# Input products of four recurrence steps at a time, accumulated in the steps' own PSUM bank and opened by a bias product

## What is computed

```python
x1 = x + (softmax(mask(q @ k.T / sqrt(32))) @ v) @ w_proj + b_proj      # q, k, v = x @ w_qkv + b_qkv, per head
for t in range(512):                                                    # all 8 sequences at once
    h = tanh(h @ Wh + x1[:, t] @ Wx + b)                                # h starts as the image row
    y[:, t] = h
out = x1 + y
```

## Time and profile before

| | us |
|---|---|
| median of 3 runs (1750.9 to 1755.51) | 1754.62 |
| the profiled execution | 1745.16 |
| its span in the trace | 1743.3 |
| TensorE busy | 1610.0 (92%) |
| VectorE busy | 884.2 (51%) |
| ScalarE busy | 707.1 (41%) |
| GpSimd busy | 151.5 (9%) |

### The profile page before, as it was taken

One profiled execution on the slowest core, in us unless ns is written; L12 is line 12 of the kernel. 1 busy time (PEld: TensorE's weight loads), 2 busy tenths in 40 slices (PEclk: granted clock), 3 DMA queues, 4 the chain that ended last, 5 costly groups with the idle time before them and its releaser, 6 DMA issues.

```text
span 1743.3 us, 67044 instructions
## 1 busy us (share of the span) xinstructions
PE 1610.0 (92%) x28908; PEld 1341.3 (77%) x28908; DVE 884.2 (51%) x2954; ACT 707.1 (41%) x2205; POOL 151.5 (9%) x248
## 2 busy tenths in 40 slices
PE   5799999989999999989999999999999998999997
PEld 4678887778787778878877787777777787888886
DVE  4345455555555555555655565556566573222222
ACT  2355555344343445444444444445445452111111
POOL 0110111010100110010101101011010100000000
PEclk8889999999999999999999999999999999999999
DMA  7656566434444465545546466556656560000000
GB/s 247 178 154 177 171 177 178 125 114 132 128 110 124 120 166 135 152 124 150 139 127 161 120 165 160 143 152 163 160 136 163 152 142 24 18 16 22 22 16 22
DMA packets 228438, 221.61 MB, mean 127 GB/s; under 512 B 22952, under 2 KB 187048, under 8 KB 227632
## 3 DMA queue, kind: packets, MB, share of 16 engines
q1 hardware_dynamic: 211568, 175.86, 37.9%
q0 software_dynamic: 16576, 41.46, 8.4%
HBM read 141.45 MB, written 75.76 MB: 125 GB/s over the span
## 4 chain that ended last, share of the span: by engine, by line
PE 76%; DVE 8%; DMA 4%; issue 4%; ACT 4%; SPq 2%; POOL 0%; DVEq 0%; POOLq 0%; ACTq 0%
PE rec L935 25%; PE turned L857 9%; PE dense L392 7%; PE dense L393 6%; PE dense L394 6%; PE scores L849 4%; PE pv L870 4%; PE scores L935 4%; PE dense L905 3%; DVE pre L762 3%; ACT hist L605 3%; PE pv L888 2%; DMA kq<-kq_dram 2%; DMA x_dram<-x1nat 1%; DVE pre L765 1%
## 5 line engine op out<-in xcount | busy, mean ns | idle before, releaser
L935 PE MATMUL rec<-wh,hist 128*8 128x128 f32 x14336 | 481.4, 275 | 63.5 <-ACT hist L605 56.5
L935 PEld LDWEIGHTS rec<-wh,hist 128*8 128x8 f32 x14336 | 353.7, 94 | 151.7 <-ACT hist L605 105.6
L605 ACT ACTIVATE hist<-pre 128x32 f32<-128x32 f32 x512 | 131.7, 257 | 587.7 <-DVE pre L772 352.3
L563 ACT ACTIVATE probs<-probs,nmax 128x128 f32<-128x128 f32 (+3 forms) x512 | 287.7, 562 | 176.0 <-DVE nmax L697 166.9
L697 DVE CUSTOM_DVE_ANT_0 probs<-scores,msk,nimg 128x128 f32<-128x128 f32 (+3 forms) x512 | 275.4, 544 | 52.2 <-PE scores L849 50.2
L762 DVE STREAM_TRANSPOSE pre<-rec 128x128 f32<-128x128 f32 x448 | 141.3, 315 | 316.2 <-PE rec L935 313.4
L857 PE MATMUL turned<-ident,probs 128*128 128x128 f32 x1280 | 241.1, 288 | 2.2 <-DVE probsT L706 1.3
L849 PE MATMUL scores<-kq 96*128 96x128 f32 (+3 forms) x512 | 202.8, 401 | 16.2 <-DMA kq<-kq_dram 15.8
L857 PEld LDWEIGHTS turned<-ident,probs 128*128 128x128 f32 x1280 | 145.2, 141 | 64.8 <-issue 54.4
L570 ACT COPY probsT<-turned 128x128 f32<-128x128 f32 (+3 forms) x256 | 107.6, 420 | 157.5 <-PE turned L857 156.3
L706 DVE COPY probsT<-turned 128x128 f32<-128x128 f32 (+3 forms) x256 | 124.6, 487 | 87.9 <-PE turned L857 87.1
(11 more groups left out here) (160 smaller groups left out, 2224.8 us busy)
## 6 DMA issues: line engine op xcount, KB each, us to landing
kq<-kq_dram SPq DMA_DIRECT2D x96, 320.0 KB, 5.0
kq<-kq_dram SPq DMA_DIRECT2D x96, 256.0 KB, 4.4
...
kq_dram<-qs_hi SPq DMA_DIRECT2D x128, 128.0 KB, 2.0
kq_dram<-ks_hi SPq DMA_DIRECT2D x128, 128.0 KB, 2.7
...
```

What stands on the lines that cost most here:

```text
L563: act.activation(probs[:, g % PROBS, 0:n], probs[:, g % PROBS, 0:n], ACT.Exp, scale=-1.0, bias=nmax[:, e, h:h + 1], accum_out=rowsum[:, e, ...
L605: act.activation(hist[:, g // HALF % 2, :, :, g % HALF], pre[:, :, 0:B], ACT.Tanh).then_inc(h_ready, 1)
L935: last = pe.matmul(d[Q * j:Q * j + B, 0:P], hist[:, before // HALF, f, :, before % HALF], wh[:, f, P * j:P * j + P], start=f == 0 and not ...
```

## The change

The products of x1 with Wx no longer go through VectorE, nor (in blocks 0 to 2) through a `dense` bank and ScalarE. They are accumulated in the bank in which the steps accumulate their state products, for a group of four steps (`GROUP`) at once: row z of each 8 x 4 rows in a column group belongs to step 4k + z. Kind "xsteps" does this for a whole group k in the attention stage, right ahead of the group's first step; "xpart" does a quarter of the next group's after each step of the tail. The bank is opened (start=True) by 4 matmuls of a row of ones (one partition, 32 columns) with the bias row `brow`, then 16 matmuls of `wx` with 32 columns of x1 accumulate. Every step then accumulates 16 matmuls with a stationary tile of 32 columns, of which 24 are zero (`state_tile`), so that it changes its own 8 rows only. VectorE only turns the bank into `pre`. ScalarE takes the tanh from every fourth column into the state tile, and once in four steps copies the four states into `hist`. All x1 is kept in `x1` by ScalarE ("keep", 4 copies of 256 columns for every trip), laid out in groups; block parity decides whether a group's 32 columns are adjacent or 128 bytes apart. `vimg` shrinks to one buffer, to make room. The weights and the lags of the order change with it: "keep" weighs nothing, and a trip's next products start ahead of it.

```diff
+GROUP = 4
+FIRST = (BLOCKS - 1) * P
...
-        last = "keep" if block_of(g) == BLOCKS - 1 else "wx"
         return ([("proj", g, c, 1.5) for c in range(C)] + [("xload", g + 2, 0, 0.0)] * (g + 2 < TRIPS)
-                + [("x1n", g, e, 0.55) for e in range(2)]
-                + [(last, g, c, 1.8 * (last == "wx")) for c in range(C)] + [("finished", g, 0, 0.0)])
+                + [("x1n", g, e, 0.55) for e in range(2)] + [("keep", g, c, 0.0) for c in range(C)]
+                + [("finished", g, 0, 0.0)])
...
-                at = max(len(side) - 3, 0)
+                at = max(len(side) - 5, 0)
...
-            if block + 1 < 2 * TRIPS:
-                emit([("vimgload", (block + 1) // 2, (block + 1) % 2, 0.0)])
+            if block < 2 * TRIPS:
+                emit([("vimgload", block // 2, block % 2, 0.0)])
...
-    ends = {g: n for n, (kind, g, _, _) in enumerate(main) if kind == "finished"}
-    begins = {}
-    for n, (kind, g, _, _) in enumerate(main):
-        if kind in ("wx", "keep"):
-            begins.setdefault(g, n)
+    begins = {g: n for n, (kind, g, i, _) in enumerate(main) if (kind, i) == ("keep", 0)}
+    ends = {g: n for n, (kind, g, i, _) in enumerate(main) if kind == "finished"}
...
     def step(t):
+        if t % GROUP == 0 and t < FIRST:
+            put("xsteps", t // GROUP, 0, 0.9)
         put("step", t, 0, 1.05)
-        if t % HALF == 1 and t > HALF:
+        if t >= FIRST and t // GROUP + 1 < S // GROUP:
+            put("xpart", t // GROUP + 1, t % GROUP, 0.2)
+        if t % HALF == 2 and t > HALF:
             put("out", t // HALF - 1, 0, 0.5)
 
     for at, (kind, g, i, w) in enumerate(main):
         put(kind, g, i, w)
         for t in place.get(at, []):
             step(t)
-    put("tail", 0, 0, 4.0)
-    for t in range((BLOCKS - 1) * P, S):
+    for c in range(C):
+        put("xpart", FIRST // GROUP, c, 0.2)
+    for t in range(FIRST, S):
         step(t)
-        clock += 1.2
+        clock += 0.7
...
+        diagonal = states[:, 1:1 + GROUP * (P + 1)].rearrange("p (s n) -> p s n", s=GROUP)[:, :, 0:P].rearrange(
+            "p s (f b z) -> p s f b z", f=C, b=B)[:, :, :, :, 0]
...
-        def rec_bank(t):
-
-            return scores[0] if t >= (BLOCKS - 1) * P and t % 2 == 0 else rec
+        def rec_bank(k):
+
+            return scores[0] if k >= FIRST // GROUP and k % 2 == 0 else rec
+
+        def state_tile(t):
+
+            s = t % GROUP
+            at = P * s if s < GROUP - 1 else P * s + GROUP
+            return states[:, at:at + P].rearrange("p (f q) -> p f q", f=C)
+
+        def state_cells(t):
+            return state_tile(t).rearrange("p f (b z) -> p f b z", z=GROUP)[:, :, :, (t + 1) % GROUP]
+
+        def x1_cells(g, f):
+
+            p, r = divmod(g, PAIRS)
+            if p % 2 == 0:
+                return x1[:, f, :].rearrange("p (m r e s) -> p r e s m", r=PAIRS, e=2, s=GROUP)[:, r]
+            return x1[:, f, :].rearrange("p (r e s m) -> p r e s m", r=PAIRS, e=2, s=GROUP)[:, r]
+
+        def x1_group(k, f):
+
+            b, m = divmod(k, P // GROUP)
+            if b % 2 == 0:
+                return x1[:, f, B * GROUP * m:B * GROUP * (m + 1)]
+            return x1[:, f, :].rearrange("p (n m) -> p n m", m=P // GROUP)[:, :, m]
...
-                elif kind == "keep":
-                    wait_copied(pool, "proj", g, C - 2)
-                    wait_copied(pool, "proj", g, C - 1)
-                    if i == 0:
-
-                        pool.wait_ge(pre_ready, STEPS * (g - PAIRS + 1))
-                    pool.tensor_copy(x1kept[:, :, r, :, i, :, :],
-                                     x1T[:, i, :].rearrange("p (e a k t) -> p a k e t", e=2, a=PAIRS, k=2)
-                                     ).then_inc(x1_kept, 1)
...
-                elif kind == "wx":
-                    wait_dense(act, kind, g, i)
+                elif kind == "keep":
+                    wait_copied(act, "proj", g, i)
                     if i == 0 and g >= PAIRS:
 
-                        act.wait_ge(pre_ready, STEPS * (g - PAIRS + 1))
-                    cells = xw[:, r, :, i] if p % 2 == 0 else xw[:, :, r, i]
-                    act.activation(cells.rearrange("p g e t -> p g e t"),
-                                   bank(kind, g, i)[:, 0:2 * P].rearrange("p (e g t) -> p g e t", e=2, g=PAIRS),
-                                   ACT.Identity, bias=bx[:, i:i + 1]).then_inc(copied(kind, g, i), 1)
+                        act.wait_ge(rec_ready, STEPS * (g - PAIRS + 1) - GROUP + 1)
+                    act.copy(x1_cells(g, i), x1T[:, i, :].rearrange("p (e m s) -> p e s m", e=2, s=GROUP)
+                             ).then_inc(x1_kept, 1)
...
                 elif kind == "step":
+                    k, s = divmod(g, GROUP)
                     act.wait_ge(pre_ready, g + 1)
-                    if g % HALF == 0 and g >= 2 * HALF:
-                        wait_dense(act, "out", g // HALF - 2, 0)
-                    act.activation(hist[:, g // HALF % 2, :, :, g % HALF], pre[:, :, 0:B], ACT.Tanh).then_inc(h_ready, 1)
+                    if s == 0 and k:
+
+                        act.wait_ge(hist_kept, k)
+                    act.activation(state_cells(g), pre[:].rearrange("p f (b z) -> p f b z", z=GROUP)[:, :, :, s],
+                                   ACT.Tanh).then_inc(h_ready, 1)
+                    if s == GROUP - 1:
+                        if g % HALF == GROUP - 1 and g >= 2 * HALF:
+                            wait_dense(act, "out", g // HALF - 2, 0)
+                        act.wait_ge(h_ready, g + 2)
+                        at = g % HALF - s
+                        act.copy(hist[:, g // HALF % 2, :, :, at:at + GROUP].rearrange("p f b s -> p s f b"), diagonal
+                                 ).then_inc(hist_kept, 1)
...
-                        trip = g // 2 - 1
-                        if block_of(trip) == BLOCKS - 1:
-                            wait_dense(dve, "x1n", trip, 1)
-                            dve.wait_ge(x1_kept, C * (trip - (BLOCKS - 1) * PAIRS + 1))
-                        else:
-                            wait_dense(dve, "wx", trip, C - 1)
+                        wait_dense(dve, "x1n", g // 2 - 1, 1)
+                        dve.wait_ge(x1_kept, C * (g // 2))
...
-                    b, s = divmod(g, P)
-                    r, s = divmod(s, STEPS)
-                    if g == (BLOCKS - 1) * P:
-                        dve.wait_ge(x1_kept, C * PAIRS)
-                        for e in range(2):
-                            dve.wait_ge(v_stored[e], 16 * TRIPS)
-                    elif g % P == 0:
-                        for c in (C - 2, C - 1):
-                            wait_copied(dve, "wx", b * PAIRS + PAIRS - 1, c)
-                    if b == BLOCKS - 1 and s == 0:
-                        set_out(r, 0)
                     dve.wait_ge(rec_ready, g + 1)
-                    dve.transpose(pre_all, rec_bank(g)[:, 0:P]).then_inc(rec_turned, 1)
-                    dve.wait_ge(rec_turned, g + 1)
-                    if b == BLOCKS - 1:
-                        dve.tensor_tensor(pre[:, :, 0:B], pre[:, :, 0:B],
-                                          bx[:].unsqueeze(2).broadcast_to([P, C, B]), ALU.add).then_inc(pre_ready, 1)
-                        if s == 0:
-                            set_out(r, 1)
-                    else:
-                        cells = xw[:, :, r, :, :, s] if b % 2 == 0 else xw[:, r, :, :, :, s]
-                        sums = pre[:, :, 0:B].rearrange("p f (b e) -> p f b e", e=2)
-                        dve.tensor_tensor(sums, sums, cells.rearrange("p a f e -> p f a e"), ALU.add).then_inc(pre_ready, 1)
+                    dve.transpose(pre_all, rec_bank(g // GROUP)[:, 0:P]).then_inc(pre_ready, 1)
...
-                elif kind == "wx":
-                    if i == 0:
-                        pe.wait_ge(weights_loaded, WEIGHT_LOADS)
-                    for f in range(C):
-                        last = pe.matmul(d[:, 0:2 * P], wx[:, f, P * i:P * i + P], x1T[:, f, :],
-                                         start=f == 0, stop=f == C - 1)
-                    last.then_inc(dense_ready, 1)
...
+                elif kind in ("xsteps", "xpart"):
+                    if g == 0:
+                        pe.wait_ge(weights_loaded, WEIGHT_LOADS)
+                        wait_bank(pe, "xsteps", 0, 0)
+                        pe.wait_ge(brow_loaded, 16)
+                    if g % (P // GROUP) == 0 and i == 0:
+                        trip = g // (P // GROUP) * PAIRS + PAIRS - 1
+                        pe.wait_ge(x1_kept, C * (trip + 1))
+                    if i == 0:
+
+                        if g == FIRST // GROUP:
+                            pe.wait_ge(shifted_ready, HEADS)
+                        elif g:
+                            pe.wait_ge(pre_ready, GROUP * (g - (g > FIRST // GROUP)))
+                        for j in range(C):
```

(30 more changed lines are left out.)

65 lines of the change are left out of this document (31 added, 34 removed).

## The result

| | us | ratio to the kernel before |
|---|---|---|
| kernel before, median of 4 runs | 1753.04 | |
| changed kernel, median of 4 runs (1768.2 to 1783.61) | 1775.38 | 1.0128 [1.0081, 1.0176] |
| the changed kernel again, on another chip, 4 runs | 1776.53 | 1.0114 [1.0058, 1.017] |
| its profiled execution and its span | 1768.2, 1766.4 | |

The change makes the kernel 22 us slower; the forecast was 1713 us, 40 us faster. The two profiled executions have spans of 1743.3 and 1766.4 us: +23.1, where the sum said -41.5. 64.6 us are to be explained.

What follows compares the result with a forecast made beforehand. The prediction took TensorE's work to bound the attention stage and a chain of burst, turn, add and tanh the tail. Its terms summed to -41.5 us, from 1754.6 to 1713 us, range 1690 to 1742.

Steps and rivals of the forecast that it cites:

- x1 products in: Attention stage: 96 groups of x1 products at 1.22 us each, one form change included, add 117.1 us.
- waits for a tanh: Attention stage: TensorE's waits for a tanh fall from 56 to 25 us, -31, anything from -15 to -45.
- width of 32 columns: Every step: a state 32 columns wide costs nothing; upper bound 0.02 us for each of 512 steps, 10 us.
- The tail's chain: Tail: without VectorE's add and its semaphore a step takes 1.80 us instead of 2.02, -27.9 us over 127 steps.
- What would show it: List of expected signs; 1.8 us three times and more at the fourth step means the group's opening is on the path.
- Into the tail: From step 383 to step 384: 2.9 us instead of 4.68, -1.8, with ScalarE's copies due before TensorE asks.
- I am near the lower end: Attention stage, price of x1 products: +117.1 us chosen between bounds of +105.6 and +192.
- rival A: x1 products cost more: strided columns and bias row at half pace, +49 us in the attention stage; chance 15%.
- wx out: Attention stage: 12 trips x 4 chunks of wx products at 1.83 us go, -87.8 us; their waits for ScalarE, -4.5.
- So this stage costs the sum of TensorE's work: Attention stage: TensorE is busy 187.8 of 200 us in a window, its waits small and mostly for a tanh.
- Rival B: Tail: TensorE's clock falls, a step then costs 0.83 us more; 8% near the old time or slower, 3% up to 1730.
- one vimg buffer: Attention stage: a single buffer costs nothing, since its load starts when a norm ends and the next is 16 heads away.

## Why the prediction was wrong, point by point

The sum against what the two profiles and the runs show, in us:

| term | forecast | measured |
|---|---|---|
| tail, steps 384 to 511, with "out" and set_out | -33.6 | -30.8 |
| into the tail and the end | -1.7 | +2.5 |
| x1 products in | +117.1 | +142.2 |
| wx products out and their waits, trips 1 to 3 | -22.0 | +3.8 (the whole stretch) |
| the same, after trip 4 | -70.3 | taken as -70.3, not measured alone |
| waits for a tanh | -31 | -34.6 |
| new waits for a turn | in the last | +4.7 |
| width of 32 columns | 0 | +5 |
| sum | -41.5 | +22.5, span +23.1 |

The term taken over can be tried by difference. From the first score of trip 4 to step 384 the changed kernel takes 50.5 us more in the first profiles (42 in the second ones); the terms that fall there come to 49.

- *The tail's chain*: right. 1.79 to 1.81 us a step at full clock. The fourth step takes 1.87, as "What would show it" said of an opening on the path; in the kernel with the row in one piece it is 1.81 too. Step 384 alone took 2.5 us, at the low clock after a wait of 2.75 us.
- *Into the tail*: wrong by 4. From the last step before it to step 384 it is 6.7 us (forecast 2.9, before 4.68). The prediction had ScalarE's copies done in time. The timeline has them at the end of the path, four of 0.6 us in a row behind a tanh and a copy into hist, and then the opening at the low clock:

```profile
1516.57 1.08 PE L934 MATMUL rec<-wh,states 128*32 128x128 f32 x32
...
1518.68 2.25 ACT L614 COPY x<-x1T 128x256 f32<-128x256 f32 x4
...
1520.98 0.64 PE L923 MATMUL scores<-vimg_rows,pimgT_rows 1*32 1x128 f32 x8 [2.75 <-ACT x L614]
1521.55 1.97 PE L927 MATMUL scores<-wx,x 128*32 128x128 f32 x32
```

- *x1 products in*: the first failed step, 25 us. "I am near the lower end" was chosen because a form change was what the rows priced. That part was right: 0.11 to 0.13 us against 0.12. (The rule on a drain that the prediction cites from the Trainium skill, TensorEngine Tiling (Array Packing), stands there in the section "Key Properties", not in the one that it names.) The strided row, which stands in rival A as the thing no row priced, was the error, 20.5 of the 25 us. Its two rounds of four matmuls start 0.216 us apart instead of 0.133, and the x1 products start 0.35 us after the second one instead of 0.22: 0.21 us in two rounds, so each takes about twice the 0.109 us of a round inside a step's burst. The Trainium skill, SBUF — State Buffer, section "Door 1: The DMA port swizzle (why `[64,N]` ≈ `[32,N]`)", has the rule for accesses that cross to a new 16-byte line; the trace agrees for the streamed row. Stationary columns are another matter: 128 bytes apart they cost 0.05 us a group (0.95 against 0.90), with a one-row product ahead of them or, in the kernel without it, none, and nothing behind a bias product of full columns (0.874 in both blocks).
- *wx out*: the second failed step, 26 us. "So this stage costs the sum of TensorE's work" was read from a window at 600 to 800 us and used for all 48 products. Twelve of them lay in trips 1 to 3, in which TensorE's work does not set the time: 22 us less of it gave the ratio 1.0003. Rival B had the mechanism, a clock that falls when TensorE has less to do, and placed it in the tail.
- *The width*: right as a bound. A step's burst to the next line's start went from 0.998 to 1.011 us in the median, 0.013 x 384 = 5 us.
- *Waits for a tanh, ScalarE, one vimg buffer*: right. The runs without the add and without the copies into hist agree with the first two, and the version changed in the tail alone has the single buffer and loses nothing in trips 4 to 12.
- *Rivals*: A was the one to heed, at 15% and with 49 us as its worst. Its half on the bias row came true (20.5 us for 96 x 0.22 = 21), its half on the columns did not (1.7 us for 28); alone it would have ended near 1738, inside the stated range. Its sign, step 384 later than 1475, came too, but it would have laid the second error at A's door as well. That two errors of one sign could add was given no chance of its own: each rival stood for itself. With a net of 6 us between +29 and -35, the stage's sign hung on two prices that no row had.
